# Expert MLP with rotation: each expert's weights loaded once, in 256 KB pieces, and split where they land

## What is computed

```python
h = gelu(x @ Wi[e] + bi[e])            # 128x512 @ 512x2048, exact gelu
o = h @ Wo[e] + bo[e]                  # 128x2048 @ 2048x512
r = o + x
y = (r - mean(r)) * rsqrt(var(r) + 1e-12) * gamma[e] + beta[e]
# groups of four features: (0,1) turned by theta[s], (2,3) by phi[s]
out = rotate(y, theta[s], phi[s])
```

## Time and profile before

| | |
|---|---|
| median of three runs | 2729.39 us |
| the profiled execution | 2733.55 us |
| its span, first to last instruction | 2731.5 us |
| TensorE matmul busy | 2671.3 us, 98% |
| VectorE, ScalarE, GpSimd busy | 72%, 35%, 49% |
| granted TensorE clock, mean | 0.996 |
| moved by DMA | 376.00 MB |

### The profile page before, as it was taken

How to read it: one execution, slowest core, us unless ns; L and a number is a source line. 1 busy time by engine, 2 the same in 40 slices (tenths; PEclk the granted TensorE clock), 3 DMA queues, 4 the chain that set the end, 5 groups by cost and what they waited for, 6 DMA issues and landing times.

```text
span 2731.5 us, 54978 instructions
## 1 busy us (share of the span) xinstructions
PE 2671.3 (98%) x12310; PEld 1207.0 (44%) x12311; DVE 1974.4 (72%) x4931; ACT 952.1 (35%) x1697; POOL 1328.5 (49%) x1560
## 2 busy tenths in 40 slices
PE   4999999999999999999999999999999999999998
PEld 2444444444444444444444444444444444444443
DVE  5777777777777777777776777777777777777776
ACT  6333333333333333333333333333333333333332
POOL 0686547860037870687500677607873687500000
PEclk9999999999999999999999999999999999999999
DMA  6867655756355854656644657546765656543442
GB/s 193 191 147 167 150 147 133 194 118 123 88 131 134 192 138 116 165 132 180 146 92 89 161 132 179 150 88 161 176 153 134 165 135 177 117 90 88 88 90 58
DMA packets 741352, 376.00 MB, mean 138 GB/s; under 512 B 682816, under 2 KB 682944, under 8 KB 732608
## 3 DMA queue, kind: packets, MB, share of 16 engines
q1 hardware_dynamic: 677136, 173.16, 34.2%
q0 software_dynamic: 27312, 135.28, 15.6%
q10 hardware_dynamic: 36864, 67.13, 7.4%
HBM read 174.13 MB, written 33.55 MB: 76 GB/s over the span
## 4 chain that ended last, share of the span: by engine, by line
PE 96%; issue 1%; DMA 1%; DVE 1%; ACT 0%; DVEq 0%; SPq 0%; ACTq 0%; POOLq 0%; POOL 0%
PE o_ps L836 48%; PE z_ps L827 48%; DMA wi<-in_L_cond_Wi 0%; DMA xT<-x 0%; DMA wo<-in_L_cond_Wo 0%; DVE wo L765 0%; DVEq L196 0%; DVE z_ps L634 0%; ACT h L445 0%; DMA hT<-in_itok_B 0%; ACT z_ps L439 0%; DVE h L644 0%; ACT wo L494 0%; DVE x L639 0%; ACT wo L509 0%
## 5 line engine op out<-in xcount | busy, mean ns | idle before, releaser
L827 PE MATMUL z_ps<-wi,xT 128*128 x6096 | 1340.1, 380 | 15.7 <-issue 12.0
L836 PE MATMUL o_ps<-wo,hT 128*128 (+1 forms) x6144 | 1347.0, 379 | 0.2 <-DMA hT<-h 0.2
L827 PEld LDWEIGHTS z_ps<-wi,xT 128*128 128x128 f16 x6096 | 596.7, 98 | 745.9 <-issue 52.3
L836 PEld LDWEIGHTS o_ps<-wo,hT 128*128 128x128 f16 x6144 | 601.2, 98 | 725.3 <-issue 0.7
L439 ACT ACTIVATE z_ps<-z_ps 128x512 f32<-128x512 f32 x512 | 298.0, 582 | 1327.0 <-DVE z_ps L634 1322.9
L644 DVE SCALAR_TENSOR_TENSOR h<-z_ps,tok,h 128x512 f16<-128x512 f32 x512 | 381.2, 745 | 102.8 <-ACT h L445 102.7
L634 DVE SCALAR_TENSOR_TENSOR z_ps<-z_ps,tok,bi_all 128x512 f32<-128x512 f32 x512 | 386.1, 755 | 64.0 <-DVE ln L675 29.8
L373 POOL TENSOR_TENSOR wi<-staged 128x512 f32<-128x512 f32 x112 | 120.7, 1078 | 616.3 <-DVE r_ps L654 605.3
L445 ACT ACTIVATE h<-z_ps,tok 128x512 f16<-128x512 f32 x512 | 351.9, 687 | 21.6
L434 ACT ACTIVATE x<-xbuf,tok 128x512 f16 (+1 forms) x128 | 92.4, 722 | 387.8 <-DVEq L617 386.2
L689 DVE SCALAR_TENSOR_TENSOR y<-r_ps,rot,y 128x128 f32<-128x128 f32 x512 | 193.3, 449 | 19.2 <-ACT y L452 4.3
(11 more groups left out here) (126 smaller groups left out, 1457.8 us busy)
## 6 DMA issues: line engine op xcount, KB each, us to landing
staged<-in_L_cond_Wi POOLq DMA_DIRECT2D x56, 1024.0 KB, 5.9
staged<-in_L_cond_Wo POOLq DMA_DIRECT2D x56, 1024.0 KB, 6.5
xbuf<-in_x ACTq DMA_DIRECT2D x128, 256.0 KB, 2.7
out<-y ACTq DMA_DIRECT2D x128, 256.0 KB, 2.4
hT<-h SPq DMA_TRANSPOSE x512, 3.1
bi_all<-in_L_cond_bi POOLq DMA_DIRECT2D x7, 1024.0 KB, 7.7
wi<-in_L_cond_Wi SPq DMA_DIRECT2D x4, 1024.0 KB, 8.6
wo<-in_L_cond_Wo POOLq DMA_DIRECT2D x4, 1024.0 KB, 5.8
```

The costliest lines, as they stand in the source:

```text
L827: last = t.matmul(z_ps[:, n, :], xT16[:, j, a, k, :], wi16[:, bass.ds(b, 1), w, k, cs], start=(k == 0 and (a, w) == PASSES[0]), stop=(k == ...
L836: last = t.matmul(o_ps[:, j, :], hT16[:, j, n, a, c, :], wo16[:, bass.ds(b, 1), w, n * GC + c, :], start=(n == 0 and c == 0 and (a, w) == ...
```

## The change

- `staged` is gone. Each weight matrix of ranks 1 to 7 is loaded once, in 16 pieces of 128 partitions by 512 float32 (256 KB), straight into the place where its hi and lo parts will stand. Four loads are in flight, each on a semaphore of its own.
- The layout of `wi16` and `wo16` is now [partition, buffer, piece, hi/lo, 512] instead of [partition, buffer, hi/lo, row block, columns], so that a piece's float32 values cover exactly its hi and lo parts. TensorE's operand slices follow; order and number of the matmuls stay.
- `split` writes the scaled value to a small tile `scaled`, copies it as float16 to hi, and subtracts for lo. Squares go to `squared` and `summed` (512 wide), so a fold starts at 256.
- The bias comes in eight pieces and bo, gamma and beta at three places, one at a time.
- Since loads now write into the weight buffer itself, a rank's first load waits for `s_res`.
- Rank 0's hi and lo parts go out as four runs of 512 instead of one run of 2048.

```diff
-        wi16 = sb("wi16", [P, 2, 2, KH, I], F16)
-        wo16 = sb("wo16", [P, 2, 2, KI, H], F16)
-        staged = sb("staged", [P, 2, QN])
+        wi16 = sb("wi16", [P, 2, NC, 2, BANK], F16)
+        wo16 = sb("wo16", [P, 2, NC, 2, BANK], F16)
+        scaled = sb("scaled", [P, BANK])
+        squared = sb("squared", [P, BANK])
+        summed = sb("summed", [P, BANK])
...
-                chain.step(g.tensor_scalar(hi, raw, scale, 1.0, ALU.mult, ALU.mult))
-                chain.step(g.tensor_scalar(raw, raw, scale, 1.0, ALU.mult, ALU.mult))
-                chain.step(g.tensor_tensor(lo, raw, hi, ALU.subtract))
+                chain.step(g.tensor_scalar(scaled[:], raw, scale, 1.0, ALU.mult, ALU.mult))
+                chain.step(g.tensor_copy(hi, scaled[:]))
+                chain.step(g.tensor_tensor(lo, scaled[:], hi, ALU.subtract))
...
+                def load(j):
+                    m, c = divmod(j, NC)
+                    k, n = divmod(c, NB)
+                    if m == 0:
+                        source = Wi[bass.ds(e, 1), k * P:(k + 1) * P, n * BANK:(n + 1) * BANK]
+                    else:
+                        source = Wo[bass.ds(e, 1), c * P:(c + 1) * P, :]
+                    pool.dma_start(raw(m, c), source.rearrange("e p n -> p (e n)")).then_inc(s_stage[j % 4], 16)
+
+                def landed(j):
+                    pool.wait_ge(s_stage[j % 4], ((r - 1) * 2 * NC // 4 + j // 4 + 1) * 16)
+
+                def sum_squares(m, c):
+                    to = squared if c else summed
+                    chain.step(g.tensor_tensor(to[:], raw(m, c), raw(m, c), ALU.mult))
+                    if c:
+                        chain.step(g.tensor_tensor(summed[:], summed[:], squared[:], ALU.add))
+
+                def matrix_scale(m):
+                    fold(summed, BANK)
...
+                if not boot:
+                    pool.wait_ge(s_res, before)
+                for j in range(4):
+                    load(j)
+                for c in range(NC):
+                    landed(c)
+                    sum_squares(0, c)
+                    load(c + 4)
+                    if c % 2:
+                        bi_piece(pool, e, b, c // 2, s_bias[b])
+                matrix_scale(0)
+                bias_scale()
+                for c in range(NC):
+                    halves(0, c)
+                    if c < NC - 4:
+                        landed(NC + c)
+                        load(NC + c + 4)
+                g.engine_nop().then_inc(s_wi, 1)
+                if not boot:
+                    pool.wait_ge(s_ln, before)
+                for c in range(NC):
+                    if c >= NC - 4:
+                        landed(NC + c)
+                    sum_squares(1, c)
+                    if c % 4 == 0 and c < 12:
+                        bgb_piece(pool, e, b, c // 4, s_bgb[b])
+                matrix_scale(1)
+                for c in range(NC):
+                    halves(1, c)
+                pool.wait_ge(s_bgb[b], (r + 1) // 2 * 48)
+                g.engine_nop().then_inc(s_wo, 1)
...
-                        last = t.matmul(z_ps[:, n, :], xT16[:, j, a, k, :], wi16[:, bass.ds(b, 1), w, k, cs],
+                        last = t.matmul(z_ps[:, n, :], xT16[:, j, a, k, :], wi16[:, bass.ds(b, 1), k * NB + n, w, :],
...
-                        last = t.matmul(o_ps[:, j, :], hT16[:, j, n, a, c, :], wo16[:, bass.ds(b, 1), w, n * GC + c, :],
+                        last = t.matmul(o_ps[:, j, :], hT16[:, j, n, a, c, :], wo16[:, bass.ds(b, 1), n * GC + c, w, :],
```

More of the change, by code:

```diff
@@ L75, in expert_mlp_rotate_kernel @@
     QN = H * I // P // Q
+    NC = H * I // P // BANK
+    CQ = NC // Q
+    BIP = I // (NC // 2)
     XB = 5
@@ L168, in expert_mlp_rotate_kernel @@
         s_bbgb = sem("s_bbgb")
-        s_stage = [sem(f"s_stage{i}") for i in range(2)]
+        s_stage = [sem(f"s_stage{i}") for i in range(4)]
         s_wi = sem("s_wi")
@@ L222, in by_rows, with half_of, bi_piece, bgb_piece @@
             return region.rearrange("p (c n) -> p c n", n=H)
+        def half_of(m, a, q):
+            return (wi16, wo16)[m][:, 0, q * CQ:(q + 1) * CQ, a, :]
         def load_bi(queue, e, b, landed):
             queue.dma_start(bi_all[:, b, :], bi[bass.ds(e, 1), :].broadcast_to([P, I])).then_inc(landed, 16)
+        def bi_piece(queue, e, b, j, landed):
+            c = slice(j * BIP, (j + 1) * BIP)
+            queue.dma_start(bi_all[:, b, c], bi[bass.ds(e, 1), c].broadcast_to([P, BIP])).then_inc(landed, 16)
+        def bgb_piece(queue, e, b, j, landed):
+            v = (bo, gamma, beta)[j]
+            queue.dma_start(bgb_all[:, b, j, :], v[bass.ds(e, 1), :].broadcast_to([P, H])).then_inc(landed, 16)
         def load_bgb(queue, e, b, landed):
@@ L300, in scales, with fold @@
                     scale_of(ss, None, [(col(NBI), 5)], chain)
[L303 to L308, removed]
+            def fold(acc, w):
+                while w > 1:
+                    w //= 2
                     chain.step(g.tensor_tensor(acc[:, 0:w], acc[:, 0:w], acc[:, w:2 * w], ALU.add))
-                    w //= 2
                 return acc[:, 0:1]
             def split(hi, lo, raw, scale):
-                chain.step(g.tensor_scalar(hi, raw, scale, 1.0, ALU.mult, ALU.mult))
-                chain.step(g.tensor_scalar(raw, raw, scale, 1.0, ALU.mult, ALU.mult))
-                chain.step(g.tensor_tensor(lo, raw, hi, ALU.subtract))
+                chain.step(g.tensor_scalar(scaled[:], raw, scale, 1.0, ALU.mult, ALU.mult))
+                chain.step(g.tensor_copy(hi, scaled[:]))
+                chain.step(g.tensor_tensor(lo, scaled[:], hi, ALU.subtract))
             pool.wait_ge(s_tables, 1)
             e0 = slot_value(pool, EXPERT, 0, E - 1)
-            raw = wo16[:, 1].rearrange("p a k n -> p (a k n)").bitcast(F32)
+            raw0 = wo16[:, 1].rearrange("p c a n -> p (c a n)").bitcast(F32)
             pool.wait_ge(s_braw[Q - 1], 16)
             for q in range(Q):
-                pool.dma_start(by_rows(raw[:, q * QN:(q + 1) * QN]), wo_quarter(e0, q)).then_inc(s_braw[Q + q], 16)
+                pool.dma_start(by_rows(raw0[:, q * QN:(q + 1) * QN]), wo_quarter(e0, q)).then_inc(s_braw[Q + q], 16)
             load_bgb(pool, e0, 0, s_bbgb)
@@ L341, in stage @@
                     else:
[L342 to L383, removed]
-                    scales(("wi", "wo")[m], pool_s[:, 0:1], b, chain)
[L385 to L399, removed]
@@ new lines, in matrix_scale, with bias_scale @@
+                def matrix_scale(m):
+                    fold(summed, BANK)
+                    chain.step(g.partition_all_reduce(pool_s[:, 0:1], summed[:, 0:1], P, ADD_LANES))
+                    scales(("wi", "wo")[m], pool_s[:, 0:1], b, chain)
+                def bias_scale():
+                    pool.wait_ge(s_bias[b], (r + 1) // 2 * 16 * (NC // 2))
+                    for n in range(NB):
+                        piece = bi_all[:, b, n * BANK:(n + 1) * BANK]
+                        chain.step(g.tensor_tensor((squared if n else summed)[:], piece, piece, ALU.mult))
+                        if n:
+                            chain.step(g.tensor_tensor(summed[:], summed[:], squared[:], ALU.add))
+                    scales("bi", fold(summed, BANK), b, chain)
@@ new lines, in halves @@
+                def halves(m, c):
+                    w = (wi16, wo16)[m]
+                    split(w[:, b, c, 0, :], w[:, b, c, 1, :], raw(m, c), wscale[:, m:m + 1])
+                if not boot:
[8 more added lines that the diff above has]
+                        bi_piece(pool, e, b, c // 2, s_bias[b])
@@ L484, in iteration @@
                     sum_x(s + 2, k)
-            raws = [w[:, 1].rearrange("p a k n -> p (a k n)").bitcast(F32) for w in (wi16, wo16)]
-            his = [w[:, 0, 0].rearrange("p k n -> p (k n)") for w in (wi16, wo16)]
-            drop = his[1].bitcast(F32)[:, 0:QN]
+            raws = [w[:, 1].rearrange("p c a n -> p (c a n)").bitcast(F32) for w in (wi16, wo16)]
+            drop = wo16[:, 0].rearrange("p c a n -> p (c a n)").bitcast(F32)[:, 0:QN]
             def squares(m, q):
@@ L732, in iteration @@
                     rotate(s - 2)
-            raws = [w[:, 1].rearrange("p a k n -> p (a k n)").bitcast(F32) for w in (wi16, wo16)]
-            his = [w[:, 0, 0].rearrange("p k n -> p (k n)") for w in (wi16, wo16)]
-            los = [w[:, 0, 1].rearrange("p k n -> p (k n)") for w in (wi16, wo16)]
+            raws = [w[:, 1].rearrange("p c a n -> p (c a n)").bitcast(F32) for w in (wi16, wo16)]
             def exponent(ss):
@@ L764, in lo_parts @@
                     dve.wait_ge(s_bhi, m * Q + q + 1)
-                    v.scalar_tensor_tensor(out=los[m][:, c], in0=raws[m][:, c], scalar=wscale[:, m:m + 1],
-                                           in1=his[m][:, c], op0=ALU.mult, op1=ALU.subtract).then_inc(s_blo, 1)
```

(5 more changed lines are left out.)

11 lines of the change are left out of this document (4 added, 7 removed).

## The result

The changed kernel took 2725.73 us (median of 20 runs, 2723.96 to 2727.94) against 2729.68 us for the kernel before (20 runs, 2726.62 to 2731.71). The ratio is 0.9984 with a 95% interval of 0.9978 to 0.9990, so 2.7 to 6.0 us faster. The forecast was 2724.5 us, with a range from 2720 to 2731. The profiled execution took 2724.80 us, 8.75 less than that of the kernel before. This is twice what the medians show, which already warns that one pair of profiles holds chance.

The account below looks back on a forecast made before the run. The prediction took TensorE to bound the kernel, with GpSimd's longer work hidden behind it at no cost. From 2729.4 us it took off 4.9 for the gap at the loop's entry: 2724.5 us, range 2720 to 2731.

Parts of the forecast that it names:

- TensorE bound, blocks unchanged: TensorE, busy 98% of the span, sets the time; its blocks of 48 matmuls stay at 10.36 us with unchanged counts.
- GpSimd's cycle, 268 us, weights in time: GpSimd's weight preparation for rank 7 grows from 238.3 to 268 us, with 32 us left before TensorE needs Wo.
- The copy: In GpSimd's split, the float32 to float16 copy for hi was taken at 0.71 us, so 0 over 32 pieces.
- The first squares: At a rank's start on GpSimd, they wait for a load ordered after the release: +5 us.
- 16 loads of 1.19: GpSimd orders 32 loads instead of 16, at a mean of 1.19 us each: +19.0 us on its cycle.
- The start's gap goes, -4.9 us: At the loop's entry, TensorE's 3.02 us gap closes to 0.17 and the next block loses its extra 1.69 us.
- The later gaps and the bound of +3 for 43 DMAs: Two later TensorE gaps might give -2.2 us, 43 DMAs per rank instead of 20 might cost +3; together taken as 0.
- The saved reading counts for nothing by itself: GpSimd's work stays hidden behind TensorE, so reading 56 MB less gains no time by itself.
- the gap stays: Rival: the loop's first code fetch or slot-value read causes the entry gap, without traffic; about 2729 us, chance 0.31.
- Small pieces crowd the transposes: Rival: smooth traffic beside all slots lengthens some 40 TensorE gaps by 0.2 us each; 2737 us, chance 0.05.
- Late weights: Rival: each of 32 loads waits 3 us, GpSimd's cycle becomes 364 us and TensorE waits; near 2986 us, chance 0.05.

Follow-up runs that it names:

- b_delay: The kernel before, with GpSimd's rank 1 held until the residual of slot 1 is done: 2729.25 us against 2729.80, ratio 1.0005.
- b_unroll: The kernel before, with slots 3 to 6 written out ahead of the hardware loop: 2728.59 us, ratio 0.9995.
- b_noprefetch: The kernel before, with the first two quarters of ranks 2 to 7 ordered only after the wait for the residual: 2730.25 us, ratio 1.0000.
- a_bias1: The changed kernel, with the bias as one DMA of 1 MB at the second piece instead of eight of 128 KB: 2725.54 us.

## Why the prediction held, and where it did not

- *TensorE bound, blocks unchanged*: right. 10.36 us a block, the same counts, in every kernel here.
- *GpSimd's cycle, 268 us, weights in time*: right, 260.4 us. The copy took 0.62 us and not 0.71 (32 pieces: -2.9). The first squares came 3.8 us after the release, not 5 (-1.2). And I added 16 loads of 1.19; of the old loads 14 stood inside the old cycle, and of the new ones 28 outside the landing time, so 14 of 1.2 more (-2.2).
- *The start's gap goes, -4.9 us*: this is the step that failed, and the time came out near it by luck. In the two profiles the gap did go (5.8 us of excess at slots 3 and 4, now 0.5). But it was one execution's chance: the same start showed 0.63 us in another kernel, and removing all traffic from it gained nothing in the median (`b_delay`, 1.0005). The slip was in the sum. The profiled execution was 4.2 us slower than the median, which is about the size of the gap, and the prediction took the 4.9 off the median, in which it was not contained. The chain from a late transpose of x to the gap was argued from what stood nearby; the row itself said "issue", and this transpose had landed 1.15 us before the gap began. A transpose did have a part in it, but one of h, by way of the queue's lead of 1.58 us.
- *The later gaps and the bound of +3 for 43 DMAs*: I cancelled them against each other and took 0. Here the real gain sat: 17.3 us of excess from slot 5 on became 13.7 (15.7 to 18.0 in `b_delay`, `b_unroll` and `b_noprefetch`, 14.9 in `a_bias1`). The move of two reads takes 19.3 us from the kernel before (2730.32 - 2711.00) and 14.5 from the changed one (2725.73 - 2711.22). 10 us of each are the quiet turns of the loop. So traffic cost 9.3 us before and costs 4.5 now: half. The term that I missed is the slot-table read, spread as 0.1 to 1 us over some 40 to 50 iterations; the queue of GpSimd carried 135 MB before and 77 MB now, 0.57 of it.
- *The saved reading counts for nothing by itself*: wrong for the same reason. It is most likely what counted, since small pieces alone did not help, the layout alone lost, prefetch and bias burst were neutral, and doubling the bytes gave back about 2.4 us of 4. This last step rests on seven of twelve runs and is not settled. A rival stays untested: the changed kernel also spreads its orders, one piece at a time behind each sum, and no run spread the old bytes like this without other changes. Why the new layout with the old loading lost 0.13% is open too; only that it acts through the reads is shown.
- *The rival "the gap stays"* had named the read of slot values as a possibility, with the traffic having no part in it. The reads are the reason of all gaps; but the traffic acts through them, and the forecast of about 2729 us did not come.
- *Small pieces crowd the transposes*: with four in flight TensorE never waits for one, though at the start the transpose of x took 5.8 us and the longest of h 8.7, more than the 3 to 5 forecast. With eight the wait is real (17.6 us).
- *Late weights*: did not occur, and 39 us are left. One correction to the description of the kernel: GpSimd's start on rank r waits for the last slot of rank r-2, the buffer's last user, and not of rank r-1. The trace of rank 7 shows it (released during iteration 100, needed in iteration 114), and the sums went by that.

In "DMA: Bandwidth & Descriptors", section on queues, rings and completion order, the Trainium skill says that the DMA engines alternate between queues packet by packet. That rule would let a transpose keep its share whatever GpSimd queues up. The traces agree with it only in part: with four pieces in flight the longest transpose at the start took 8.7 us, with eight 17.6, against medians of 3.2 and 3.1.

## What to carry to other kernels

When the bounding engine shows gaps whose reason is "issue", look at what its own queue does there (register reads, asserts, branches) before looking for a late buffer; parting four table reads into two and two was worth 0.7% in the kernel before and 0.5% in the changed one, against 0.16% for the whole change. Before building on a gap of one profile, ask whether it is in the median: a profiled execution that is slower than the median by about the gap is a warning, and an unchanged stretch in a second kernel's profile tells at once. And taking traffic away can pay on an engine that never waits for it.

## What was new about the hardware

- A queue's read of one value from SBUF mostly took 0.30 us, in a quiet turn too with one of 0.64 among four. Three of four within 10 us of an order of 2 MB took 0.62, 0.95 and 0.99 us; the longest in the kernel before was 1.23. Four in a row with what stands around them outlast the 3.5 to 3.9 us that TensorE's queue is ahead of its array, two do not, even at a loop's turn.
- A wait for a transpose 12 matmuls before these reads cut that lead to 1.58 us, and a stop of 0.23 us was followed by one of 3.02.
- A stop of TensorE for 3.0 us was followed by a block with 1.7 us more at a granted clock of 0.66, one of 1.46 us by none.
- With up to eight DMAs of 256 KB in flight a transpose took 17.6 us to land, against a median of 3.1. In the kernel before, with 2 MB ordered at 71 us and 2 more 10 us later, one of x took 10.9 and one of h 12.7. In the changed kernel the longest at this place took 8.7.
